# Softmax scaling of an audio tower's attention: one two-scalar VectorE operation in place of GpSimd

## What is computed

```
h = relu(einsum('blfd,fd,fdk->blk', windows(x), filt, W_k) + b_k)      # 8 taps, 248 windows, 64 features
q, k, v = (layernorm(h) @ W.T + b for each of q, k, v)
mask = (q[:, :, 0] != 0) & (k[:, :, 0] != 0)                           # one flag per row (query)
prob = where(mask, softmax(where(mask, q @ k.T / 8, -1e9)), 0)         # 248 x 248 per sequence
h = h + (prob @ v) @ Wo.T + bo
h = h + sum over the top 2 of 8 experts of weight * (relu(layernorm(h) @ W1 + b1) @ W2 + b2)
```

## Time and profile before

| | |
|---|---|
| median of 3 runs | 343.15 us (342.94 to 343.67) |
| span of the profiled execution, first to last instruction | 340.8 us |
| PE busy | 307.6 us (90%) |
| DVE (VectorE) busy | 248.6 us (73%) |
| ACT busy | 240.9 us (71%) |
| POOL (GpSimd) busy | 92.8 us (27%) |
| of POOL: L330, p times rmask | 32 x 1014 ns = 32.4 us |
| chain that ended last | PE 40%, DVE 22%, issue 16%, ACT 11%, DMA 7%, POOL 0% |
| mean granted TensorE clock | 0.959 of full speed |

### The profile page before, as it was taken

One profiled execution on the slowest core, in us unless ns is written; L12 is line 12 of the kernel. 1 busy time (PEld: TensorE's weight loads), 2 busy tenths in 40 slices (PEclk: granted clock), 3 DMA queues, 4 the chain that ended last, 5 costly groups with the idle time before them and its releaser, 6 DMA issues.

```text
span 340.8 us, 6412 instructions
## 1 busy us (share of the span) xinstructions
PE 307.6 (90%) x1486; PEld 188.0 (55%) x1486; DVE 248.6 (73%) x824; ACT 240.9 (71%) x545; POOL 92.8 (27%) x85
## 2 busy tenths in 40 slices
PE   8587799999999999999999999999999999979754
PEld 8264657565645657475656556474656565534220
DVE  2574747879696979779786969697887979492823
ACT  2427497969686887879686978778786969764520
POOL 1103031513232241515122322315151323132302
PEclk9767899999999999999999999999999999999985
DMA  6120214070614225160706142241707060504050
GB/s 181 50 61 0 63 58 124 17 182 5 159 37 124 73 78 119 29 168 5 191 1 151 45 130 67 81 116 26 171 9 187 2 164 0 147 21 126 12 136 15
DMA packets 17228, 28.38 MB, mean 83 GB/s; under 512 B 3264, under 2 KB 13760, under 8 KB 17216
## 3 DMA queue, kind: packets, MB, share of 16 engines
q1 hardware_dynamic: 16928, 27.98, 32.6%
q10 hardware_dynamic: 288, 0.28, 0.2%
HBM read 21.90 MB, written 2.29 MB: 71 GB/s over the span
## 4 chain that ended last, share of the span: by engine, by line
PE 40%; DVE 22%; issue 16%; ACT 11%; DMA 7%; SPq 1%; DVEq 1%; ACTq 0%; POOL 0%
PE bank_a L787 11%; DMA cb<-weights 5%; DVE ts L252 4%; PE bank_y L846 4%; PE bank_s L897 4%; PE bank_h L836 3%; PE bank_h L837 3%; ACT p L367 3%; ACT hid L376 2%; PE bank_b L904 2%; PE bank_s L804 2%; DVE hsum L637 2%; DVE acc L548 2%; DVE gw L617 2%; PE bank_h L867 2%
## 5 line engine op out<-in xcount | busy, mean ns | idle before, releaser
L376 ACT ACTIVATE hid<-bank_h,col 128x496 f32<-128x496 f32 x128 | 84.0, 674 | 10.5 <-PE bank_h L837 9.2
L846 PE MATMUL bank_y<-hid,w_sb 128*64 128x496 f32 x256 | 68.0, 612 | 3.6 <-DVE acc L548 3.6
L836 PE MATMUL bank_h<-xs,w_hi 128*128 128x496 f32 x128 | 56.2, 439 | 3.0 <-DVE xs L253 2.4
L548 DVE SCALAR_TENSOR_TENSOR acc<-bank_y,col,cb 128x496 f32<-128x496 f32 x64 | 45.4, 730 | 17.3 <-DMA cb<-weights 9.8
L837 PE MATMUL bank_h<-xs,w_lo 128*128 128x496 f32 x128 | 49.8, 389 | 0.0
L262 POOL TENSOR_TENSOR total<-acc 128x496 f32<-128x496 f32 x16 | 20.1, 1256 | 106.7 <-DVE acc L548 106.7
L330 POOL TENSOR_TENSOR p<-p,rmask 124x496 f32<-124x496 f32 x32 | 32.4, 1014 | 51.9 <-DVE rmask L564 51.8
L265 POOL TENSOR_TENSOR total<-total,acc 128x496 f32<-128x496 f32 x16 | 20.0, 1250 | 70.5 <-DVE acc L548 70.5
L836 PEld LDWEIGHTS bank_h<-xs,w_hi 128*128 128x128 f32 x128 | 24.3, 190 | 13.4 <-issue 7.1
L718 DVE SCALAR_TENSOR_TENSOR h<-bank_s,col,h 128x248 f32<-128x248 f32 x16 | 7.6, 476 | 31.9 <-PE bank_s L897 31.9
L367 ACT ACTIVATE p<-bank_s,nmax 124x248 f32<-124x248 f32 x64 | 29.4, 466 | 0.3 <-DVE nmax L555 0.2
(11 more groups left out here) (105 smaller groups left out, 584.8 us busy)
## 6 DMA issues: line engine op xcount, KB each, us to landing
cb<-weights SPq DMA_DIRECT2D x64, 248.0 KB, 4.5
kk<-kk SPq DMA_DIRECT2D x16, 248.0 KB, 2.9
x<-xt SPq DMA_DIRECT2D x15, 256.0 KB, 2.9
out<-h SPq DMA_DIRECT2D x16, 124.0 KB, 1.8
w_sb<-w SPq DMA_DIRECT2D x3, 256.0 KB, 3.6
wtok_sb<-wtok SPq DMA_DIRECT2D x1, 256.0 KB, 2.7
x<-xt ACTq DMA_DIRECT2D x1, 256.0 KB, 3.9
weights<-ct_sb SPq DMA_DIRECT2D x16, 15.5 KB, 1.4
```

What stands on the lines that cost most here:

```text
L376: act.activation(hid[2 * (p % 2) + s][:, :], bank_h[s][:, 0:TOK], ACT.Relu, bias=col[:, C_B1 + e:C_B1 + e + 1]).then_inc(hid_ready[s], 1)
L548: dve.scalar_tensor_tensor(out=acc[p % 2][:, :], in0=bank_y[p % 2][:, 0:TOK], scalar=col[:, C_B2 + p:C_B2 + p + 1], in1=cb[:, p, :], op0=A ...
L836: pe.matmul(bank_h[e % 2][:, 0:TOK], w1_hi[:, e, :], xs[par][:, :], start=True, stop=False)
L846: last = pe.matmul(bank_y[p % 2][s * D:s * D + D, 0:TOK], w2_sb[:, 2 * p + s, :], hid[2 * (p % 2) + s][:, :], start=True, stop=True)
```

## The change

`scale` moves from GpSimd to VectorE. One `tensor_scalar` multiplies by two per-partition scalars, `rsum` and `mask`, and since each of these has one column per i, a tile takes two instructions of 124x248. `rmask`, its product and its semaphore go away, and so does the wait of `recip` for the scaling before it. `scale(c, 0)` stands at the very end of VectorE's iteration, behind `both_weights`; `scale(n, 1)` stands right behind `recip(n, 1)`, ahead of `normalise(c)`.

```diff
@@ GpSimd
-            def scale(n, b):
-
-                pool.wait_ge(rm_ready, 2 * n + b + 1)
-                pool.tensor_tensor(p_sb[b][0:HALF, :, :], p_sb[b][0:HALF, :, :],
-                                   rmask[0:HALF, b, :].unsqueeze(2).to_broadcast([HALF, 2, WIN]),
-                                   ALU.mult).then_inc(p_ready, 1)
-
             def iteration(t, odd, d_, c_, n_, m_, f_):
...
                 if f_:
                     add(pool, f, 2)
-                if n_:
-                    scale(n, 0)
-                    scale(n, 1)
                 if d_:
@@ VectorE
             def recip(n, b):
                 dve.wait_ge(ex_ready, 2 * n + b + 1)
-                after(dve, p_ready, 2 * n + b - 1)
                 dve.reciprocal(rsum[0:HALF, b, :], psum_p[0:HALF, b, :]).then_inc(rs_ready, 1)
+
+            def scale(n, b):
+
                 dve.wait_ge(rs_ready, 2 * n + b + 1)
                 dve.wait_ge(mask_ready, n + 1)
-                dve.tensor_tensor(rmask[0:HALF, b, :], rsum[0:HALF, b, :], mask[0:HALF, :, b],
-                                  ALU.mult).then_inc(rm_ready, 1)
+                for i in range(2):
+                    last = dve.tensor_scalar(p_sb[b][0:HALF, i, :], p_sb[b][0:HALF, i, :], rsum[0:HALF, b, i:i + 1],
+                                             mask[0:HALF, i, b:b + 1], ALU.mult, ALU.mult)
+                last.then_inc(p_ready, 1)
...
                 if n_:
                     recip(n, 1)
+                    scale(n, 1)
                 if c_:
                     normalise(c)
...
                     recip(c, 0)
                 if n_:
                     both_weights(n)
+                if c_:
+                    scale(c, 0)
```

More of the change, by code:

```diff
@@ L120, in audio_tower @@
         rsum = sb("rsum", [128, PAIR, 2])
-        rmask = sb("rmask", [128, PAIR, 2])
         p_sb = [sb(f"p{b}", [128, 2, WIN]) for b in range(PAIR)]
@@ L194, in audio_tower @@
         rs_ready = sem("rs_ready")
-        rm_ready = sem("rm_ready")
         p_ready = sem("p_ready")
@@ L325, in _ @@
             pool.memset(eps[:, :], EPS).then_inc(set_pool, 1)
-            def scale(n, b):
-                pool.wait_ge(rm_ready, 2 * n + b + 1)
-                pool.tensor_tensor(p_sb[b][0:HALF, :, :], p_sb[b][0:HALF, :, :],
-                                   rmask[0:HALF, b, :].unsqueeze(2).to_broadcast([HALF, 2, WIN]),
-                                   ALU.mult).then_inc(p_ready, 1)
             def iteration(t, odd, d_, c_, n_, m_, f_):
-                d, n, m, f = t + 2, t, t - 1, t - 2
+                d, m, f = t + 2, t - 1, t - 2
                 if f_:
                     add(pool, f, 2)
-                if n_:
-                    scale(n, 0)
-                    scale(n, 1)
                 if d_:
```

## The result

The changed kernel is slower. Its median is 347.94 us (19 runs, 344.25 to 352.56), beside 343.97 us (19 runs) for the kernel before on the same chip: a ratio of 1.0095, 95% interval 1.0071 to 1.012, some 3.3 us. The ratio leaves out four executions of the changed kernel (349.45 us and more, the profiled one among them) that lie more than 1.5% above its fastest. The prediction said 340.2 us and faster, with 347.0 as its high end.

The account below looks back on a forecast made before the run. PE, nearly full, was taken as the bound, reached through the start of `x_lo`. Six pairs gaining 0.51 us each (-3.1), t = 0 (-0.2) and the tail (+0.3, +0.1) gave -2.9: 343.15 to 340.2 us, range 337.8 to 347.0.

Parts of the forecast that it names:

- what bounds the kernel, and the stall: PE is close to full; VectorE's L252 (`ts`) stands still behind POOL's late `x_lo`, lasting 1.31 and 1.25 us against 0.41.
- The price of the new operation: Each scaling on VectorE takes 0.35 us, 0.27 of DVE's time after overlap; ends 0.29 and 0.47.
- The fast rate: The scaling on VectorE runs faster than L252's one element a cycle, giving 0.35 us instead of 0.47.
- Taken back by the spread weights: Later L707 delays the output's DMA and `cb` behind it; loses 0.13 us in the plain and 0.07 in the loop turn.
- The lock goes the other way: Rival: in every loop turn the second scaling stands still behind POOL's `x_lo`, L904 +0.77 us; 347.7 us, chance 0.13.
- at about 18.7 us: Sign of being right: the loop turn's period falls to this from 19.10 us.
- the plain turn some 0.3 shorter: Sign of being right: the other kind of turn also shortens, its L904 put 0.27 us sooner.
- The sum: A pair of turns gains 0.51 us, six pairs 3.1; with head and tail -2.9 in total, giving 340.2 us.
- What covers the added DVE work is the stall that goes: Plain turn: scalings add 0.22 and 0.40 us on VectorE, yet L904 comes 0.27 sooner as L252 no longer waits.
- The won time is lost again: Rival: PE is 96% busy and the `cb` chain may be worse, losing 0.25 us more a turn; 343.2 us, chance 0.16.
- One element a cycle: Rival: each scaling on VectorE takes 0.47 us, 0.39 of DVE's time; 346.0 us, chance 0.08.

Follow-up runs that it names:

- b_tlo: The kernel before, with `x_lo` on GpSimd made to wait for the low half of `ts` (`tlo`); 341.66 us, ratio 0.9903.
- a_one_x: a_xlo with the scaling by `rsum` alone, the product with the mask left out; 343.5 us, ratio 0.9965.
- a_mt: The changed kernel with `x_lo` waiting for the low half of `ts` and `masks(c)` moved behind `indices(n)`; 342.82 us, ratio 0.9945.
- a_tlo: The changed kernel with `x_lo` on GpSimd made to wait for the low half of `ts` (`tlo`); 346.12 us, ratio 1.0029.
- a_xlo: The changed kernel with `x_lo` on GpSimd made to wait until both scalings are done; 345.74 us, ratio 1.0042.
- a_masks: The changed kernel with `masks(c)` moved from behind `normalise_2(n)` to behind `indices(n)`; 354.62 us, ratio 1.0286.
- a_outp: a_tlo with the output's store issued from GpSimd's queue, ahead of `x_lo`, instead of SyncE's; 359.5 us, ratio 1.0419.
- b_mtp: The kernel before with `x_lo` waiting for `tlo`, the masks moved behind `indices(n)` and the output's store on GpSimd's queue; 348.93 us, ratio 1.0106.

## Why the prediction was wrong

**Right: what bounds the kernel, and the stall.** "So DVE's operation with two SBUF operands stood still while POOL worked", and `x_lo` "late for no reason of its own": L250 lasts 0.41 us in all but the first three turns, `x_lo` starts 0.08 after `x_hi`, and b_tlo, which removes this alone, gains 3.3 us. The chain from `xn` to L904 was put at 2.30 us and is 2.29 (166.44 to 168.73). L707 was put 1.96 us before L904, by 160.46 and 162.42, and stands there in all twelve turns of the loop. POOL's 60 us are 61.4. Two smaller signs were off: `x_lo` was to start 0.1 to 0.3 after `x_hi`, and DVE to be busier by 1 us an iteration; it is 0.5 (8.3 us in 16).

**Wrong in size: "The price of the new operation", 0.35 us.** I added the 0.06 for a pointer scalar once, though the operation has two; it is 0.404, within the stated ends (0.29 and 0.47). By a_one_x, 0.06 an operation makes 2.6 us of time; so I estimate that the missing 0.054 made about 2.3, with the wide interval of that run. The fast rate itself was right. The Trainium skill (VectorE: DVE Perf Modes, the perf-mode tier table) has the double rate and nothing for pointer scalars; the estimate by that alone, 0.29, is further off than mine: the runs show 0.06 us for each.

**Wrong: "Taken back by the spread weights", +0.13 and +0.07.** This is the step that failed by most, by the medians; the intervals do not tell it from the price of the operation. I followed the later `cb` from `acc` to the `xn` of L659, and there the sum was nearly right (6.13 us after L904 by 168.55 and 162.42; measured 6.0 to 6.6). But I stopped there. The next instruction is `kmask`, had its mean at 348 ns for four columns, and I used that very row as evidence for the fast rate, writing that it "stands still behind POOL". It stands behind POOL's `total`, which the first two `acc` release. Moving `acc` by 0.5 us relative to the turn moves `total`, and `kmask` goes from 0.29 or 0.42 to as much as 0.78 us. Price by a_mt against a_tlo: 2.9 us. That is the whole stall; the part that was there before, 348 of the 622 ns, is in it, so that what the forecast left out is somewhat less.

**Wrong: "The lock goes the other way", chance 0.13, all or nothing.** The mechanism was right and its price nearly: the scaling stands still behind `x_lo`, and `xn` comes 1.09 us later (put: 1.21, by 180.26 and 179.05). Three things were wrong. It was to happen in every loop turn or in none, and it happens in some turns, in the profiled execution in three of twelve. It may widen the spread of the runs, 344 to 352 us, but does not explain all of it: a_xlo, where no scaling is long, spreads over 344 to 349. It was to happen in the loop turn, yet apart from the first (t = 2, lost) the loop turns are safe, their scaling 0.21 to 0.25 us ahead of `x_lo`, while the plain turns stand within 0.02 of the edge. By the prediction's own numbers a plain turn's second scaling starts at 159.85, 0.21 ahead of `x_lo` at 160.06, and I did not look at it; measured are 0.075 to 0.091. What I lacked was the common start: both lists hang on one `rowmax`, so that the distance is the same in every plain turn and a small edit on either list moves them all. And the edge lies not 0.08 behind the end of `x_hi` but at it: starts 0.075 ahead of `x_lo` lost, starts 0.081 ahead won. In the median the lost turns cost 1.8 us (the change against a_xlo). I named the near tie and could have said that a difference of 0.15 us between two numbers known to 0.27 is a coin, not a 0.13.

The rule of the Trainium skill (SBUF — State Buffer, "Who interferes with whom"), whoever issues first keeps the ports for its whole instruction, is borne out in kind by the long scaling and by the stretched `x_lo`. By the rows, first is not read from the recorded starts as they stand: VectorE needs to be 0.08 us ahead. That may be no more than how the records overlap: each second scaling is recorded from 0.083 to 0.086 before the first one's end, and the edge lies at that end. An `x_lo` that starts 0.009 us or more before it goes ahead of the second scaling, one that starts 0.003 before it or later goes behind. These rows cannot tell the two readings apart.

**The period "at about 18.7 us", "the plain turn some 0.3 shorter".** That loop turn came out at 19.12, and the plain turns without a long scaling at 18.4 to 19.2. With the lock and `kmask` taken out (a_mt) they are 18.73 and 18.54. What was left to the forecast pair of 36.96 us is 0.3, about what 0.054 for each of the eight scalings of a pair would make (0.43 at most, an estimate).

**The sum.** The kernel that the forecast's sum describes, with neither `ts` nor a scaling standing still, is a_tlo: it is 1.0 us slower than before (0.1 faster to 2.1 slower) where the sum says 2.9 faster. So the sum failed without the lock too, in its premise "What covers the added DVE work is the stall that goes": the stall is worth 3.3 us (b_tlo), and the work with what it sets off costs 4.3 (b_tlo to a_tlo). From the forecast of -2.9 us to the measured +3.3 are 6.2 us. The three terms give 2.3 + 2.9 + 1.8 = 7.0, each uncertain by 1.5 us or so. In the other direction, from kernel to kernel: before to b_tlo -3.3, b_tlo to a_tlo +4.3, a_tlo to the change +2.3, together the measured +3.3. So the change costs 4 us of VectorE work and waits behind it, wins 3.3 by getting out of `x_lo`'s way, and loses about 2 to the lock. These are differences of the measured ratios; that they add is assumed. The profiled execution has 4.6 us on top of its median, of which its three lost turns can be no more than 3.3; its granted clock from 25 to 50 us was also lower than before, 0.73 of full speed against 0.86 (a mean over time at 2.4 and at 1.2 GHz). Over the 19 executions the four longest have a mean clock of 0.939 to 0.946 and the shortest 0.977. How the rest divides was not tried.

"The won time is lost again" (343.2, 0.16) was nearest to the mechanism, `cb`, but not to the place or the size. "One element a cycle" (0.08) fell with the 0.404. No case had two faults at once, and the range ended at 347.0 because I let the high end be a single rival; the ratio, put on the 343.15 us from which the prediction started, gives 346.4, just inside it.

## What to carry to other kernels

An operation is not moved off GpSimd for free even when GpSimd's turn is what hurts: first ask whether the instruction that does the harm can be placed where VectorE waits anyway. Here one semaphore wait in front of `x_lo` gave 3.3 us and moving two small operations another 2.2, where moving the scaling cost 3.3. Where a VectorE and a GpSimd instruction that stand still for each other start within some 0.1 us, order them by a semaphore, or else an edit elsewhere can flip every turn (a_masks, +6.6 us). Look for the event from which both lists start: the same distance then comes back every turn. And when a transfer comes later, follow it through the GpSimd instruction that it releases to the small VectorE operation which that one holds up; when a store is moved, look for who waits to overwrite its source.

## What the hardware showed that I had not expected

- Which engine goes first and which stands still: over the changed kernel and a_masks, a second scaling that started 0.081 us or more ahead of GpSimd's recorded start ran in 0.40 us, one that started 0.075 ahead or later took 1.35 to 1.49 us. The loser, when it is GpSimd, shows it too: 1.44 to 1.46 us instead of 1.28.
- Width does not protect: `kmask` with 124x4 stands for up to 0.78 us behind GpSimd, and so does `gw` in both kernels. The view of one tile, changed kernel:

```profile
L609 DVE TENSOR_TENSOR gw<-eg,gw x16: 154/663/1244, 46.3 to 329.8; 124x4 f32<-124x4 f32 x16
```

 It is 0.16 us without a neighbour on POOL; in the changed kernel the one at 181.42 lasts until 182.10, 0.02 behind POOL's `total` (L263), and all but the first of the 16 last 0.62 us or more. No run moves it, so what these 0.5 us a turn cost is open.
- The time of the wait lies in the recorded duration of the VectorE instruction, not in idle time ahead of it: an instruction whose mean differs from that of its form elsewhere is where to look.
- A per-partition scalar costs 0.06 us each in a `tensor_scalar` of 124x248: 0.404 with two, 0.344 with one, and 0.29 with none, which is an estimate by the casts of the earlier trace rows.
- A store of 124 KB takes 1.8 us to land from SyncE's queue, and 4.2 (a_outp) or 3.6 (b_mtp) from GpSimd's, by medians. How much of it is GpSimd's own work and how much a wait behind VectorE was not tried.
